# A perceiver layer on one core: context and half of the key weights loaded first, nine matmuls of ones, means and scan 0 moved up, and work of the tail moved off VectorE

## The reference

```python
x = x + xattn(layernorm(x), ctx, mask, Wq, Wkv, Wproj, bproj)      # 16 heads of 16, 64 queries, 256 keys, 16 batches
x = x + mamba(layernorm(x), ...)                                   # in_proj to 2 x 512, conv of 4 taps, silu, scan of 16 states, gate, out_proj
x = x + bitffn(layernorm(x), w_gate, w_up, w_down)                 # 256 -> 1024 -> 256

def scan:   h = exp(delta * A) * h + delta * B * x ;  y = sum_n(h * C) + x * D
def bitffn: gate = silu(bitlinear(x, w_gate)); up = bitlinear(x, w_up); return bitlinear(gate * up, w_down)
def bitlinear(x, w):   # x is rounded to 8 bits with one scale a row, w to -1, 0, 1 with one scale (mean of |w|)
    return round(x * 127 / max|x|) / (127 / max|x|) @ w_quant.T
```

## Time and profile before

| | |
|---|---|
| median of 3 runs | 412.8 us (412.78 to 412.99) |
| profiled execution, its own time | 412.8 us |
| its span, first to last instruction | 411.0 us |
| PE busy | 356.3 us (87%) |
| DVE busy | 346.9 us (84%) |
| POOL busy | 285.5 us (69%) |
| ACT busy | 278.5 us (68%) |

### The profile page before, as it was taken

The page is one execution under the profiler, slowest core; times in us unless marked ns, Lnnn a source line. Parts: engine busy times, 40 slices in busy tenths (PEclk is TensorE's granted clock), DMA queues, the critical chain, the costliest instruction groups (busy, mean ns, idle before and its releaser), DMA issues.

```text
span 411.0 us, 8655 instructions
## 1 busy us (share of the span) xinstructions
PE 356.3 (87%) x2864; PEld 241.3 (59%) x2868; DVE 346.9 (84%) x723; ACT 278.5 (68%) x596; POOL 285.5 (69%) x333
## 2 busy tenths in 40 slices
PE   3889999998998999985898999898899778789684
PEld 1557767574766674553465566566666556457352
DVE  1468888778889787968999999989999999988795
ACT  1266679758975895289879879767874553265564
POOL 0046475646557563237999999999999699976820
PEclk9999999999999999999999999999999999999989
DMA  5981010101010000008600000375000000000001
GB/s 192 383 350 53 1 53 3 53 13 41 12 43 2 2 3 0 0 6 230 181 2 0 2 5 26 88 190 134 2 0 2 1 2 0 2 0 2 13 27 65
DMA packets 22623, 22.41 MB, mean 55 GB/s; under 512 B 1042, under 2 KB 20242, under 8 KB 22068
## 3 DMA queue, kind: packets, MB, share of 16 engines
q1 hardware_dynamic: 22020, 21.39, 16.5%
q10 hardware_dynamic: 560, 0.48, 0.3%
HBM read 20.75 MB, written 1.12 MB: 53 GB/s over the span
## 4 chain that ended last, share of the span: by engine, by line
PE 33%; DVE 24%; issue 15%; ACT 13%; POOL 12%; DMA 1%; DVEq 0%; POOLq 0%; PEldq 0%; ACTq 0%
DVE both L1591 9%; POOL both L1885 8%; PE ps L536 8%; PE ps L505 4%; PE ps L750 3%; PE ps L488 3%; PE ps L740 3%; ACT both L1172 2%; DVE both L1415 2%; PE ps L523 2%; PE ps L566 2%; ACT both L1007 2%; PE ps L553 2%; ACT both L1158 1%; PE ps L599 1%
## 5 line engine op out<-in xcount | busy, mean ns | idle before, releaser
L1885 POOL TENSOR_TENSOR both<-both 128x1024 f32<-128x1024 f32 x64 | 149.4, 2367 | 0.2
L1591 DVE TENSOR_TENSOR_SCAN both<-both,ps 128x1024 f32<-128x1024 f32 x64 | 142.7, 2271 | 4.6 <-PE ps L740 4.6
L1831 POOL TENSOR_SCALAR both<-both,rden 128x256 f32<-128x256 f32 x128 | 62.0, 500 | 62.9 <-DVE rden L1422 62.9
L1172 ACT ACTIVATE both<-delta,a_neg 128x504 f32<-128x504 f32 x120 | 74.8, 704 | 11.0 <-DVE both L1591 11.0
L750 PE MATMUL ps<-con,both 128*128 128x128 f32 x512 | 72.0, 279 | 7.8 <-POOL both L1885 7.6
L1007 ACT ACTIVATE both<-both,negmax 128x256 f32<-128x256 f32 x128 | 63.3, 498 | 17.9 <-DVE negmax L1415 17.9
L750 PEld LDWEIGHTS ps<-con,both 128*128 128x128 f32 x512 | 56.1, 141 | 30.0 <-issue 16.0
L740 PE MATMUL ps<-both 32*128 32x256 f32 x512 | 45.7, 426 | 10.3 <-DVE both L1591 7.8
L1415 DVE CUSTOM_DVE_ANT_0 both<-ps,both 128x256 f32<-128x256 f32 x128 | 46.9, 417 | 6.7 <-PE ps L488 5.5
L536 PE MATMUL ps<-both 128*128 128x512 f32 x64 | 34.0, 656 | 8.2 <-DMA both<-in_ctx_t 6.8
L505 PE MATMUL ps<-con,both 128*128 128x128 f32 x256 | 38.2, 275 | 0.0
(11 more groups left out here) (149 smaller groups left out, 607.6 us busy)
## 6 DMA issues: line engine op xcount, KB each, us to landing
both<-bounce SPq DMA_DIRECT2D x16, 512.0 KB, 6.3
both<-in_ctx_t SPq DMA_DIRECT2D x8, 512.0 KB, 3.5
both<-in_wg SPq DMA_DIRECT2D x1, 1024.0 KB, 8.3
both<-in_wu SPq DMA_DIRECT2D x1, 1024.0 KB, 10.8
both<-in_wd SPq DMA_DIRECT2D x1, 1024.0 KB, 12.8
win_sb<-in_win SPq DMA_DIRECT2D x1, 1024.0 KB, 14.7
resid<-in_x SPq DMA_DIRECT2D x1, 896.0 KB, 6.5
both<-in_wkv SPq DMA_DIRECT2D x1, 512.0 KB, 4.4
```

The costliest lines, as they stand in the source:

```text
L1172: act.activation(da[sl % 2].rearrange("p (a s n t) -> p a s n t", a=GT, n=HN, s=2)[:, :, :, n, 1:L], delta[:, idx % RING_D].rearrange("p ( ...
L1591: dve.tensor_tensor_scan(h_sb[:, hu % RING_H], da[e.slot % 2][:, e.tt * HU:(e.tt + 1) * HU], bank(inflow_bank(hu), 2), 0.0, ALU.mult, ALU. ...
L1831: pool.tensor_scalar(s, s, rden[:, u, q:q + 1], 1.0, ALU.mult, ALU.mult).then_inc(normed, 1)
L1885: pool.tensor_tensor(g_sb[:, hu % RING_G].rearrange("p (n s t) -> p s n t", n=HN, s=2), h_sb[:, hu % RING_H].rearrange("p (s n t) -> p s n ...
```

## The change

At the start: SP loads the context first, then only the keys' half of `wkv`; the values' half, the mask of tile 0, the next context and the rest of the mask follow. The weights of queries have a semaphore of their own. PE begins with nine matmuls of ones, ahead of its `start`; DVE's memsets and ACT's first two loads stand ahead of theirs. In tile 3 the matmul for the means goes ahead of the scores. Where the scans begin, `copy_ut(1)` and `u_of(2)` go behind scans 0 and 1, and `u_of(3)` behind scan 2.

x2 is no longer added on DVE: PE adds `resid` by a fifth matmul with the identity, and ACT copies two tiles at a time (`copy_x2`). The outputs of tiles 0 to 5 are scaled by ACT (`scale_down`) and added by POOL (`add_rows`); tiles 6 and 7 stay on DVE. The norms of tiles 3 to 7 go from POOL to ACT, POOL keeps their small factors (`offset_input`). The scale of the up part goes into `product`, which takes one small instruction out of `inner_scale`. ACT loads silu's table before it waits for the first gates.

```diff
             load_ctx(Tile(0, 0))
-            sp.wait_ge(loaded_first, N_FIRST)
+            sp.dma_start(wkv_sb[:, :, 0:D], wkv_rows[:, :, 0:D]).then_inc(loaded_kv, 16)
             sp.wait_ge(ctx_loaded[0], 16)
-            sp.dma_start(mask_sb[:], mask).then_inc(loaded_mask, 16)
+            sp.dma_start(wkv_sb[:, :, D:2 * D], wkv_rows[:, :, D:2 * D]).then_inc(loaded_wv, 16)
+            sp.dma_start(mask_sb[:, 0:TK], mask[:, 0:TK]).then_inc(loaded_mask, 16)
             load_ctx(Tile(0, 1))
...
         def _(pe):
+            pe.wait_ge(consts, 1)
+            for _ in range(WARM):
+                pe.matmul(bank(7)[:, 0:P], ones[:], ones[:], start=True, stop=True)
             start(pe, PE)
...
+                if tile.t == W_MEAN and u == 5:
+                    pe.wait_ge(w_abs, count(6))
+                    pe.wait_ge(y1_ready, count(tile.t))
+                    pe.matmul(bank(4)[:, 0:6], ones[:], wsum[:], start=True, stop=True).then_inc(w_sum, 1)
                     if last:
...
             def out_proj_of(g, tt, k):
...
-                                   wout_sb[:, c], start=c == 0, stop=c == NC - 1)
+                                   wout_sb[:, c], start=c == 0, stop=False)
+                mm = pe.matmul(bank(k)[:, tt % 2 * D:(tt % 2 + 1) * D], ident, resid[:, g * GT + tt], start=False, stop=True)
                 mm.then_inc(outproj_ready, 1)
...
+            def copy_x2(g, half):
+
+                act.wait_ge(outproj_ready, count(g * GT + 2 * half + 2))
+                t = g * GT + 2 * half
+                act.activation(resid[:, t:t + 2].rearrange("p t d -> p (t d)"), bank(SPARE_BANK if g == 0 else 3),
+                               ACT.Copy).then_inc(x2_ready, 2)
...
-            slot(12)
+            half_slot(12, 0)
+            copy_x2(0, 0)
             stage_xc(7, (x2_ready, 2))
+            half_slot(12, 1)
             slot(13)
...
+            def scale_down(t):
+
+                act.wait_ge(f_down, count(t + 1))
+                act.wait_ge(f_os, count(t + 1))
+                act.wait_ge(stored[t % 2], count(t // 2 * 16))
+                act.activation(f_o[t % 2][:], f_down_ps(t), ACT.Copy, scale=f_s2[t][:, C_OUT:C_OUT + 1]).then_inc(f_scaled, 1)
+
+            act.activation(f_warm[:], eps[:], ACT.Silu).then_inc(passed, 1)
...
-            copy_ut(1, 1)
-            u_of(2)
             for hu in range(NHU):
                 scan(hu)
                 if hu == 0:
+                    copy_ut(1, 1)
                     copy_late_gate()
+                if hu == 1:
+                    u_of(2)
+                if hu == 2:
                     u_of(3)
...
-                if hu == 47:
-                    add_scan(0, 0)
-                if hu == 59:
-                    add_scan(0, 1)
...
+            def add_rows(t):
+
+                pool.wait_ge(f_scaled, count(t + 1))
+                pool.tensor_tensor(f_o[t % 2][:], f_o[t % 2][:], resid[:, t], ALU.add).then_inc(f_out_pool, 1)
```

More of the change, by code:

```diff
@@ L61 @@
 NT_ACT = 3
+WARM = 9
+NT_POOL = 6
 PE, ACTE, DVE, POOL, SP = "tensor", "scalar", "vector", "pool", "sync"
@@ L622, in body @@
                         scores(nxt, 0, 2 if nxt.last() else 4)
-                    if tile.t == W_MEAN and u == 5:
-                        pe.wait_ge(w_abs, count(6))
-                        pe.wait_ge(y1_ready, count(tile.t))
-                        pe.matmul(bank(4)[:, 0:6], ones[:], wsum[:], start=True, stop=True).then_inc(w_sum, 1)
                     if not last:
@@ L950, in _ @@
             out_proj_of(1, 3, 3)
+            down(0)
             turn_input(4, 4)
-            down(0)
             gates(4)
@@ L955, in _ @@
             activations(2)
+            down(1)
             turn_input(5, 4)
-            down(1)
+            gates(5)
             activations(3)
-            gates(5)
             up(5)
@@ L1282, in _ @@
             round_input(1)
+            copy_x2(0, 1)
             copy_input(0, SPARE_BANK)
@@ L1319, in _ @@
             copy_yz(1, 0, 2)
+            normal_input(3)
             silu_gate(2)
@@ L1322, in _ @@
             round_inner(1)
+            copy_yz(1, 2, 2)
+            copy_x2(1, 0)
             round_inner(2)
             copy_input(3, 4)
-            copy_yz(1, 2, 2)
             copy_inner(0)
+            copy_yz(1, 3, 2)
             silu_gate(3)
-            copy_yz(1, 3, 2)
+            normal_input(4)
+            copy_x2(1, 1)
             copy_inner(1)
+            normal_input(5)
             round_inner(3)
@@ L1332, in _ @@
             silu_gate(4)
+            scale_down(0)
             copy_inner(2)
+            normal_input(6)
             copy_input(5, 4)
+            scale_down(1)
             copy_inner(3)
@@ L1337, in _ @@
             round_inner(4)
+            normal_input(7)
             copy_input(6, 4)
+            scale_down(2)
             silu_gate(6)
@@ L1342, in _ @@
             copy_inner(4)
+            scale_down(3)
             silu_gate(7)
@@ L1345, in _ @@
             copy_inner(5)
+            scale_down(4)
+            round_inner(7)
             copy_inner(6)
-            round_inner(7)
+            scale_down(5)
             copy_inner(7)
@@ L1352, in _ @@
         def _(dve):
-            start(dve, DVE)
             dve.memset(ones[:], 1.0).then_inc(consts, 1)
@@ L1358, in _ @@
             dve.memset(bank(4), 0.0).then_inc(consts, 1)
+            start(dve, DVE)
             def ln_first(n, tile, src, src_sem, src_val):
@@ L1986, in _ @@
             rounded_to_bf16(2)
-            normal_input(3)
+            offset_input(3)
             round_input(3)
```

120 lines of the change are left out of this document (59 added, 61 removed).

## The result

The changed kernel takes 419.5 us (median of 4 executions, 417.4 to 420.6), the kernel before 412.8 (411.2 to 413.0): a ratio of 1.0161, 95% interval 1.0131 to 1.0191. It is 1.6% slower. The forecast was 416.3, slower, with a range of 411.5 to 420.0. The profiled execution took 420.6, so its sum has to explain 7.8 us against the 412.8 of the earlier trace rows; the median asks for 6.7.

A forecast was written before the change was run, and what follows sets the result against it. No engine was taken to bound the kernel throughout. Start -2.8, means -1.4, scan 0 0, first half of x2 +1.7 and tail +6.0 summed to +3.5 us, span 414.5, time 416.3 us; range 411.5 to 420.0.

The forecast's parts named there:

- the waits for x2: In the tail ACT waits for PE's longer projections before copying x2: gates(3) +2.3 us, gates(4) +4.3.
- the start: Kernel start: earlier keys and a clock raised by the nine matmuls, -2.8 us (bounds -3.6 and +2).
- The forecast case: Whole kernel: tail and x2 late, start gained, 413.6 to 418.5 us, chance 0.55.
- rival 2: Start: PE's increments come only after the nine matmuls, context load at 5.8, total 420.0 us; chance 0.13.
- scan 0: Where the scans begin: DVE's new order changes nothing, POOL being busy; 0 us (bounds -0.5, +0.5).
- the first half of x2: Slot 12: ACT's decays wait for the longer projection, scan 48 starts later; +1.7 us (bounds -0.7 and +2).
- the tail: From POOL's last product to the end: ACT's waits and queue delay gates and output, +6.0 us (bounds +3.5, +7.5).
- means: Tile 3: DVE's idle 1.57 us for the matmul of means goes, -1.4 us (bounds -1.6, -0.5).
- The early increment: Start: PE's sequencer passes the queued matmuls, so the increment comes perhaps 0.7 us later and the load starts near 2.3.
- The last term: End of the tail: output(7) writes tile 5's buffer, whose rows POOL adds late before a 2.2 us store; +0.6 us.
- rival 3: Tail: PE's pauses grow, the clock falls oftener; slow time cost at most 1 us, twice that gives 418.3; chance 0.07.
- Rival 1: Tail: DVE is the bound and is relieved, ACT's waits fall into its idle time, 404.9 us; chance 0.13.

The follow-up runs named there:

- b_start_no_ones: The kernel before with the changed start (order of loads, memsets and starts) but without the nine matmuls of ones: 412.5 us.
- a_scan0_back: The changed kernel with the old order where the scans begin, copy_ut(1) and u_of(2) ahead of scan 0: 418.7 us.
- a_x2_late: The changed kernel with the tail's second copy, copy_x2(1, 1), moved on ACT behind copy_inner(1), normal_input(5), round_inner(3) and copy_input(4): 418.7 us.
- a_out_dve: The changed kernel with outputs 0 to 5 on DVE again, without scale_down on ACT and add_rows on POOL: 418.5 us.
- a_x2_dve: The changed kernel with x2 added on DVE again, projections of four matmuls and slot 12 undivided: 413.8 us.
- a_x2_out_dve: The changed kernel with both x2 and all outputs on DVE again: 413.9 us.
- b_start_means: The kernel before with the changed start, nine matmuls of ones included, and the matmul for the means ahead of tile 3's scores: 409.8 us.
- b_ones13: b_start_means with four more matmuls of ones behind PE's start: 410.0 us.
- b_ones13_product: b_ones13 with the scale of the up part taken into product and inner_scale without its third instruction: 408.3 us.

## Why the prediction was right, and where it was off

The direction and the two main mechanisms, the waits for x2 and the start, held: 416.3 was forecast, 419.5 came, inside the range. That it is inside is in part luck. The forecast case itself ended at 418.5, and the upper bound of 420.0 was rival 2's number, the late increment, which did not happen; the profiled execution, 420.6, lies outside. Of the five terms three left their own bounds: scan 0 (0.5), the first half of x2 (2) and, by a tenth, the tail (7.5). The signs named beforehand are there: scores before 13, no idle time for the means, POOL idle 4.74 before its first statistics, ACT idle 1.62 and 3.65 ahead of its two copies, gates(4) at 22.3. By its own terms, with the profiled execution's numbers:

| term | forecast | measured |
|---|---|---|
| start | -2.8 | -3.1 at the first scores, -2.4 from the second tile on |
| means | -1.4 | -1.4 |
| scan 0 | 0 | +1.0 on DVE (and 0.2 lost ahead of it) |
| first half of x2 | +1.7 | +2.9 |
| tail | +6.0 | +7.6 |
| sum | +3.5 | +7.8 |

**The start.** The early increment, the step that the rows had left open, is shown by the load at 1.99. The Trainium skill (TensorE: Matmul & The Clock Gate, table at the top) gives TensorE a queue of 64 instructions; the trace agrees: 18 rows of matmuls and as many weight loads stood ahead of the increment, and it came before most of them had run. But the split of the term was wrong: without the nine matmuls (`b_start_no_ones`) the keys started 0.8 earlier than before, where 0.5 was taken, and the second piece of keys took 1.88 in place of 2.73, so 1.8 came without them and 1.3 with them, where 2.3 was taken. Nor is it a steady gain: three of the nine traces with nine matmuls have it not. And 0.6 went to a load that the new order makes late. The forecast had called the later loads hidden.

**Scan 0** is the step that failed. The prediction argued from POOL, which has no gap from 196 to 320, and found nothing to lose. But POOL waits for DVE after 320 (the 3.08 of the earlier trace rows), so DVE's place is what counts, and DVE lost 1.0 us: `u_of(2)` was put beside a product of POOL. The traces show this by the durations, and `a_scan0_back` by their return to 0.68; its median does not show the 1.0. The Trainium skill (SBUF — State Buffer, "Summary: rules for kernel authors") says that when DVE has two SBUF inputs while a GpSimd operation reads SBUF, the second one to issue blocks until the first ends; the rows agree: `u_of(2)` started at 193.12, POOL's product ended at 191.91 + 2.36 = 194.27, and `u_of(2)` ended at 194.83, 0.56 later. The rule would have given this term beforehand.

**First half of x2.** The wait for the projection with the decays behind it was right in place and size: 0.4 before scan 46 and 1.55 before scan 48 make 2.0, against 1.7. The other 0.9 came before scan 50, where PE runs at half the clock after a pause of 2.1 us: the window from 316.5 above. Four traces have this order of slot 12 and the pause: the two whose clock fell 2.3 us behind scan 48 (the changed kernel and `a_scan0_back`) lost 0.9 before scan 50, the two whose clock fell 3.7 and 4.1 us behind it (`a_x2_late`, `a_out_dve`) lost nothing. `a_x2_dve` takes the whole 2.9 away.

**The tail.** gates(3) +2.1 (forecast 2.3), gates(4) +3.9 (4.3), product(7) 19.1 us after gates(4) (18.7). `a_x2_dve` shows that x2 on ACT, waits and fifth matmul together, is the cause of the first two: it brings gates(4) back to 18.3. That tile 7's scale on DVE would hold up gates(7) was right (PE idle 2.32 at 400.59), but the 19.1 agrees with the 18.7 by luck, for 1.5 of it is the low clock. The last term was wrong in kind: output(7) did not wait for the store of tile 5, but for PE (2.16 idle at 416.11). At full clock the part behind product(7) takes 11.7 (`a_x2_late`) against before's 10.9, and 11.4 with the outputs on DVE (`a_x2_out_dve`). The forecast had no stretch at half the clock in the tail, and there were two. Those matmuls took 0.87 and 0.62 longer at 402.24 and 403.95 and 0.6, 0.4 and 0.3 longer after 411.77, some 2.9 us together, against 0.7 for before's single one (its 46.8 against the 46.1 of `b_start_no_ones`, which has none).

So 2.2 in the tail (an estimate from these durations) and 0.9 at scan 50 are rival 3, the clock, which had been given 0.07 and 2 us at most as a case of its own. Its price came from a misreading: with two levels, a mean of 0.91 over 20 us is 3.6 us at half the clock, not 1.8 (the trace has 3.4, from 391.3). It was not a case beside the others but came on top of them. At scan 50 the new wait brings it: the clock fell there in all four traces with the changed slot 12 and in none of the ten others. In the tail this is not shown: `b_start_means` and `b_ones13`, which have none of the new waits, ran 6.8 us of it at half the clock, as long as the changed kernel. To the forecast sum of 3.5 come 3.1 for the clock, 1.0 for scan 0, 0.4 for the start, 0.2 lost ahead of the scans and 0.3 for slot 12's wait, and the tail without the clock is 0.6 below its term (5.4): 7.9, and 7.8 was measured. Rival 1 (DVE relieved) is out: DVE waits 3.32 us for PE ahead of product(7). That the outputs moved off it neither cost nor gave anything once x2 was on DVE says the same.

Open: how norms, order and the low clock share what `a_x2_out_dve` still loses in the tail; none was run alone. It is 2.6 against before, and 4.2 against `b_ones13_product` (45.2), which has the same `product` but the old norms and order.

## What to carry to other kernels

Before work is moved to an engine with idle time, look at what its in-order queue would wait for: here the copies of x2, 0.6 us each, and the matmul ahead of them moved gates(4) by 4 us, by the queue behind their waits. Judge an edit by the engine that is waited for at the next joint (DVE at 320), not by the one that is busy on the way. Of what was tried, the new start with thirteen matmuls, the means and the scale in `product` together make a kernel of 408.3 us, 1.1% below before (interval 0.8% to 1.35%); the start alone (with nine) was not clear of the noise.
